# VectorE roots for the first and last norms, an early dummy partition maximum, and experts loaded in halves

## The chip, the cores and the metric

The kernel runs on one core of a Trainium2 chip. The metric is the device time of one execution in microseconds, and the figure given for a kernel is the median of its runs. The trace is of one further execution, recorded by the hardware profiler.

## What is computed

The reference applies four residual blocks to `x` (4 x 256 tokens of 128), each after a layer norm. Weights are 128 wide.

```
x = x + tanh(g_xattn[0]) * attention(norm(x), ctx)      # softmax(q k^T) v, 64 context rows a batch
x = x + tanh(g_ffn[0])   * experts(norm(x))             # 8 experts, the best 2 of each token, gelu
x = x + tanh(g_xattn[1]) * linear_attention(norm(x), ctx)   # 16 heads of 8, softmax over q and over k
x = x + tanh(g_ffn[1])   * quantised_ffn(norm(x))       # each stage scaled by max|.| over ALL tokens
norm(x) = (x - mean) / sqrt(var + 1e-5)
```

The layer norm needs one reciprocal square root for each token. The quantised block needs the largest absolute value of five whole tensors ("x", "g", "u", "p", "o") before it can go on with each.

## The kernel before

Every engine has its own instruction stream, written out by hand in order, and the engines meet only at semaphores. The 1024 tokens are worked on in two halves of 512 (4 tiles of 128), so a norm has a number n from 1 to 8: block (n-1)//2, half (n-1)%2.

A norm goes over four engines. VectorE computes `statistics` (bn_stats L557, bn_aggr L560, then var + eps, L562). GpSimd computes the root as a power of -1/2 in `rstd_of` (L311, a 128x4 tensor_tensor). VectorE takes `shift` (L568) and normalises two tiles (L573). ScalarE normalises the other two (L404). TensorE transposes them (`normalised`, L1000), and ScalarE copies them out (L395, or as `xhi` for the second block). `keep_warm` (L993) issues matmuls on zeros between.

The start: SyncE issues the DMAs of x half 0, packa, x half 1, packb, lpbq and experts (L275 to L280). GpSimd fills `ident`, `ones` and `neg_half`, makes the identity with an affine select (L316), and only then raises `const_ready`, on which TensorE waits with its first real matmul (L1070). VectorE runs the statistics of both halves, then both `normalise` calls (L685 to L689), then `weight_scales` (L586 to L590), `scores(0)` (L601, L602), `weight_values` (L595), `scores(1)`, then `add_attention` (L608 to L615) and the statistics of the second block.

Experts: ScalarE copies each of eight 128x512 expert blocks to a high part (`high_weights`, L410), and GpSimd subtracts that from the block (`low_weights`, L327). GpSimd's order is low_weights 0 to 6, rstd_of(3), low_weights 7, rstd_of(4), then the masks and constants (L335 to L350), and last `const_late`. VectorE's `route(0)` (L639 and on) waits for `const_late`; TensorE's `gate_columns` (L1144) waits for route, `first_rows` (L1151) for that, and the expert loop for those.

The end: GpSimd runs rstd_of(7), rstd_of(8) and then `partition_all_reduce` (L384) once for each of the five maxima. VectorE takes the maxima of the normalised tokens (L825) and of each partition (L840); the reduced maximum gives the scale (L879, L880), ScalarE rounds (L503), VectorE splits (L885, L887), and TensorE runs twelve units of three matmuls (L1013, L1014, L1017). ScalarE copies six of them (L508), and VectorE takes their maxima (L870).

Of the kernel before, what the change touches and what calls it, by code (L numbers as in the profile page):

```python
# [8 lines left out]
HALVES = 2  # L9
# [4 lines left out]
EXPERTS = 8  # L14
# [11 lines left out]
ROUND = 1.5 * 2.0 ** 23  # L26

# [10 lines left out]
def build(nc, x, packa, packb, rows, experts, lpbq, gates, out):  # L38
# [5 lines left out]
    i16, u16 = mybir.dt.int16, mybir.dt.uint16  # L44
# [5 lines left out]
    with ctx:  # L50
# [31 lines left out]
        ones = sb("ones", [128, 256])  # L82
        zero16 = sb("zero16", [128, 512], f16)
# [32 lines left out]

        smax = sb("smax", [128, HALVES, TILES])
# [60 lines left out]
        def third(t, dt=None):  # L178
# [30 lines left out]
        table_load = sb("table_load", [1, 2])  # L209


        x_in = [sem(f"x_in{h}") for h in range(HALVES)]
        pa_in, pb_in, row_in, exp_in, lpbq_in, out_done = map(
            sem, ("pa_in", "pb_in", "row_in", "exp_in", "lpbq_in", "out_done"))
        const_ready, const_late, pool_step = map(sem, ("const_ready", "const_late", "pool_step"))
        dve_step, zero_ready = map(sem, ("dve_step", "zero_ready"))
# [56 lines left out]
        def _(sp):  # L273
# [4 lines left out]
            sp.dma_start(pb[:, :], packb).then_inc(pb_in, 16)  # L278
            sp.dma_start(wq4[:, :, :], lpbq).then_inc(lpbq_in, 16)
            sp.dma_start(wexp[:, :], experts).then_inc(exp_in, 16)  # L280
# [16 lines left out]
        def _(pool):  # L297
# [7 lines left out]
            def link(ins):  # L305
                pool.wait_ge(pool_step, step(ins))

            def rstd_of(n):
# [4 lines left out]
            pool.memset(ident[:, :], 0.0)  # L313
            pool.memset(ones[:, :], 1.0)
            link(pool.memset(neg_half[:, :], -0.5))
            link(pool.affine_select(out=ident[:, :], in_=ident[:, :], compare_op=ALU.not_equal, fill=1.0,  # L316
                                    base=0, pattern=[[-1, 128]], channel_multiplier=1))
            pool.drain().then_inc(const_ready, 1)
            pool.memset(v1[:, :, D:D + 1], 1.0)
            pool.iota(number[:, :], pattern=[[1, EXPERTS]], base=0, channel_multiplier=0,  # L320
                      allow_small_or_imprecise_dtypes=True)
            rstd_of(1)
            rstd_of(2)
# [6 lines left out]
            for e in range(7):  # L330
                low_weights(e)
            rstd_of(3)
            low_weights(7)
            rstd_of(4)
            link(pool.memset(first_row[:, :], 0.0))  # L335
# [45 lines left out]
            rstd_of(8)  # L381
# [7 lines left out]
        def _(act):  # L389
# [18 lines left out]
            def high_weights(e):  # L408
                act.wait_ge(exp_in, 16)
                act.activation(w_hi[e], wexp[:, e * 512:(e + 1) * 512], ACT.Copy).then_inc(we_high, 1)  # L410
# [11 lines left out]
            high_weights(0)  # L422
            evac(half(xT, 1), bank[7][:, :], xT_mm, 2, xT_ready)
            for h in range(HALVES):
                act.wait_ge(s_sub, h + 1)
                act.activation(sc[:, h, :, :], sc[:, h, :, :], ACT.Exp).then_inc(pr_ready, 1)
                high_weights(1 + h)
                if h == 0:
                    evac(v0[:, :, :].rearrange("p b d -> p (b d)"), bank[3][:, 0:256], v0_mm, 1, v0_ready)
                evac(prT[:, h, :, :].rearrange("p t d -> p (t d)"), bank[2 + h][:, 0:256],  # L430
                     prT_mm, h + 1, prT_ready)
            for e in range(3, EXPERTS):
                high_weights(e)
# [105 lines left out]
        def _(dve):  # L539
# [10 lines left out]
            dve.memset(zero16[:, :], 0.0).then_inc(zero_ready, 1)  # L550
            dve.sem_inc(gated, CREDIT)
            dve.sem_inc(lo_done, CREDIT)

            def statistics(src, h):
# [7 lines left out]
                dve.tensor_scalar(var[:, h, :], mv[:, h, :, 1], LN_EPS, None, ALU.add).then_inc(var_ready, 1)  # L562

# [124 lines left out]
            normalise(xin, 1)  # L688
            normalise(xin, 2)  # L689
# [5 lines left out]
            weight_scales()  # L695
            dve.wait_ge(tg_ready, 1)
            scores(0)
            weight_values()
# [129 lines left out]
            statistics(x4, 1)  # L828
            dve.wait_ge(xn_ready, 7)
            dve.wait_ge(xn_act, 7)  # L830
            tokens_max(0, tiles(xn, 0))
            normalise(x4, 8)
# [151 lines left out]
        def _(pe):  # L984
# [90 lines left out]
            mm(bank[5][:, 0:256], A("wq", D), kT[:, :], start=True, stop=True).then_inc(wqk_mm, 1)  # L1075
            normalised(bank[6], 1)
# [229 lines left out]
```

## Time and profile before

| | us |
|---|---|
| median of 3 runs | 166.34 (166.28 to 167.22) |
| profiled execution, its own time | 166.24 |
| span of its trace | 164.5 |
| TensorE busy | 126.1 |
| VectorE busy | 127.0 |
| ScalarE busy | 94.0 |
| GpSimd busy | 34.0 |

The span runs from the first to the last recorded instruction; 1.74 us of the execution's own time lie outside it. Rows of the timeline give start, duration, engine, line, operation, output and input, count, and in brackets the idle time before them with what ended it. "issue" there means that the profile shows nothing that the engine waited for.

### The profile page before, as it was taken

To read this page: it belongs to the slowest core of one execution; us is meant where nothing else is said; L and a number is where in the kernel's file an instruction comes from. 1 tells how busy PE (TensorE), PEld (TensorE's weight loads), DVE (VectorE), ACT (ScalarE), POOL (GpSimd) and SP (SyncE) were. 2 spreads that over 40 slices of the span, in tenths; PEclk is the share of its full clock that TensorE was granted. 3 is DMA by queue.
4 is the path that set the end of the run, shared out by engine and by line. 5 is a ranking of instruction groups with operands and counts; after the bars stand their busy time and mean duration, and the time that the engine had idled before them with its cause. 6 is when DMAs were issued, how large, how long until landed. Compare 5 with 4: busy or idle time off the path is not lost.

```text
span 164.5 us, 2167 instructions
## 1 busy us (share of the span) xinstructions
PE 126.1 (77%) x684; PEld 95.4 (58%) x684; DVE 127.0 (77%) x335; ACT 94.0 (57%) x163; POOL 34.0 (21%) x64
## 2 busy tenths in 40 slices
PE   6139998499889999999999987989809950007792
PEld 4035865288448888888886756779607830005650
DVE  1608895747879999999998875878336799989894
ACT  3006692322778888888888945242433589491380
POOL 1041679593000000000000249624000000000000
PEclk9956999969999999999999999999965997555999
DMA  4990000000033214321300000000000000000003
GB/s 157 345 413 12 0 4 2 0 0 0 0 134 123 91 49 129 126 74 59 127 0 0 0 2 2 4 2 0 0 0 4 0 0 0 0 0 0 0 0 128
DMA packets 2957, 8.17 MB, mean 50 GB/s; under 512 B 249, under 2 KB 1273, under 8 KB 2818
## 3 DMA queue, kind: packets, MB, share of 16 engines
q1 hardware_dynamic: 2944, 8.03, 13.7%
q8 instruction: 5, 0.08, 0.2%
q14 instruction: 6, 0.05, 0.1%
q10 hardware_dynamic: 2, 0.00, 0.0%
HBM read 7.48 MB, written 0.56 MB: 49 GB/s over the span
## 4 chain that ended last, share of the span: by engine, by line
PE 35%; DVE 24%; issue 16%; POOL 15%; ACT 7%; POOLq 1%; DVEq 0%; ACTq 0%
PE bank L1013 9%; PE bank L1017 9%; PE bank L1014 9%; POOL we_lo L327 4%; POOL rstd L311 3%; DVE amax_u L870 2%; DVE hidden L902 2%; DVE amax_p L875 2%; DVE stats L557 2%; ACT wexp L531 2%; POOL q_soft L376 2%; POOL wT_lo L370 2%; PE bank L1151 1%; DVE amax_g L870 1%; DVE xn L573 1%
## 5 line engine op out<-in xcount | busy, mean ns | idle before, releaser
L993 PE MATMUL bank<-zero 128*128 128x256 f16 x199 | 30.8, 308 | 17.2 <-ACT ng L527 15.1
L993 PEld LDWEIGHTS bank<-zero 128*128 128x128 f16 x199 | 21.3, 110 | 24.8 <-ACT ng L527 15.5
L455 ACT ACTIVATE hidden<-bank 128x512 f32<-128x512 f32 x32 | 19.2, 598 | 6.5 <-PE bank L1017 6.5
L733 DVE TENSOR_TENSOR low_parts<-hidden,high_parts 128x512 fp32r<-128x512 f32 x32 | 21.9, 686 | 0.1
L311 POOL TENSOR_TENSOR rstd<-var,neg_half 128x4 f32<-128x4 f32 x8 | 8.1, 1018 | 63.8 <-DVE var L562 63.8
L460 ACT ACTIVATE high_parts<-hidden 128x512 fp32r<-128x512 f32 x32 | 20.0, 624 | 1.5 <-DVE hidden L726 1.4
L1017 PE MATMUL bank<-low_parts,we_hi 128*128 128x512 f32 x32 | 12.7, 396 | 0.7 <-DVE low_parts L733 0.6
L1013 PE MATMUL bank<-xhi,we_hi 128*128 128x512 f32 x32 | 12.8, 400 | 0.0
L1013 PE MATMUL bank<-high_parts,we_hi 128*128 128x512 f32 x32 | 12.7, 395 | 0.0
L1017 PE MATMUL bank<-xlo,we_hi 128*128 128x512 f32 x32 | 12.5, 390 | 0.0
L1014 PE MATMUL bank<-xhi,we_lo 128*128 128x512 f32 x32 | 12.5, 390 | 0.0
L1014 PE MATMUL bank<-high_parts,we_lo 128*128 128x512 f32 x32 | 12.5, 389 | 0.0
L726 DVE TENSOR_TENSOR hidden<-hidden,q_exp 128x512 f32<-128x512 f32 x16 | 11.1, 691 | 1.2 <-ACT q_exp L471 0.4
L327 POOL TENSOR_TENSOR we_lo<-wexp,we_hi 128x512 fp32r<-128x512 f32 x8 | 10.4, 1324 | 6.2 <-ACT we_hi L410 6.2
L726 DVE TENSOR_TENSOR hidden<-hidden,q_soft 128x512 f32<-128x512 f32 x16 | 11.1, 691 | 0.8
L568 DVE SCALAR_TENSOR_TENSOR shift<-mv,rstd 128x4 f32<-128x4 f32 x8 | 2.3, 284 | 9.5 <-POOL rstd L311 9.4
L1013 PE MATMUL bank<-xhi,wT_hi 128*128 128x512 f32 x12 | 5.8, 484 | 4.2 <-DVE xhi L885 4.2
L404 ACT ACTIVATE xn<-stream,shift,rstd 128x128 f32<-128x128 f32 x12 | 5.3, 485 | 6.6 <-DVE shift L568 6.5
L1000 PE MATMUL bank<-ident,xn 128*128 128x128 f32 x32 | 6.0, 298 | 3.8 <-DVE xn L573 3.6
L557 DVE BATCH_NORM_STATS2 stats<-stream 128x6 f32<-128x128 f32 x24 | 5.2, 280 | 3.6 <-DMA stream<-in_x 3.5
L1017 PEld LDWEIGHTS bank<-low_parts,we_hi 128*128 128x128 f32 x32 | 6.0, 188 | 2.7 <-DVE low_parts L733 1.5
L1000 PEld LDWEIGHTS bank<-ident,xn 128*128 128x128 f32 x32 | 3.9, 154 | 5.4 <-DVE xn L573 4.4
(225 smaller groups left out, 284.1 us busy)
## 6 DMA issues: line engine op xcount, KB each, us to landing
wexp<-in_experts SPq DMA_DIRECT2D x1, 2048.0 KB, 10.5
q_soft<-gates SPq DMA_DIRECT2D x4, 512.0 KB, 3.5
q_exp<-gates SPq DMA_DIRECT2D x3, 512.0 KB, 3.7
wq<-in_lpbq SPq DMA_DIRECT2D x1, 576.0 KB, 6.1
stream<-in_x SPq DMA_DIRECT2D x2, 256.0 KB, 3.7
out<-hidden SPq DMA_DIRECT2D x2, 256.0 KB, 2.1
pa<-in_packa SPq DMA_DIRECT2D x1, 325.0 KB, 3.3
pb<-in_packb SPq DMA_DIRECT2D x1, 256.0 KB, 4.8
```

Source lines behind the costliest of these rows:

```text
L311: pool.tensor_tensor(rstd[:, h, :], var[:, h, :], neg_half[:, :], ALU.pow).then_inc(rstd_ready, 1)
L327: pool.tensor_tensor(w_lo[e], wexp[:, e * 512:(e + 1) * 512], w_hi[e].bitcast(f32), ALU.subtract)\
L455: act.activation(ge[j % NB][:, :], bank[4 + j % NB][:, :], ACT.Gelu).then_inc(gelu_done, 1)
L460: act.activation(h_hi[j % NB][:, :], hm[j % NB][:, :], ACT.Copy).then_inc(hi_done, 1)
L557: m = step(dve.bn_stats(stats[:, h, t, :], src[:, h * TILES + t, :]))
L726: dve.tensor_tensor(hm[j % NB][:, :], ge[j % NB][:, :], half(gate_rows[(j // 4) % 2], (j // FC) % 2), ALU.mult)\
L733: dve.tensor_tensor(h_lo[j % NB][:, :], hm[j % NB][:, :], h_hi[j % NB][:, :].bitcast(f32), ALU.subtract).then_inc(lo_done, 1)
L993: mm(bank[b][:, 0:256], zero16[:, 0:128], zero16[:, 0:256], start=True, stop=True)
L1000: last = pe.transpose(dst[:, t * 128:(t + 1) * 128], src[:, h * TILES + t, :], ident[:, :])
L1013: mm(dst, whi, xh, start=start, stop=False)
L1014: mm(dst, wlo, xh, start=False, stop=False)
L1017: return mm(dst, whi, xl, start=False, stop=stop)
```

## The change

GpSimd no longer makes the identity; VectorE builds it in 32x32 blocks at the start and signals `ident_ready`, on which TensorE waits only ahead of `normalised(1)`. `const_ready` now comes with the memset of `ones`. The roots 1, 2 and 8 are computed on VectorE by nine small chained instructions; `normalise(1)` moves ahead of the statistics of half 1, and `normalise(8)` ahead of `tokens_max(0)`. A dummy `partition_all_reduce` on a constant tile stands between rstd_of(7) and the five real ones. The experts come in two DMAs, ahead of lpbq. GpSimd's low_weights are ordered 2, 3, 3 around rstd_of(3) and rstd_of(4), and GpSimd waits for `xn_ready` 3 and 4 ahead of the second and third group. ScalarE makes two high parts instead of one after each exponential. `weight_scales` moves behind `scores(0)`.

```diff
+MAGIC = float(0x5F3759DF)
+RS = 0.375 ** 0.5
...
 @@ sync
+            for k in range(2):
+                part = slice(k * EXPERTS * 256, (k + 1) * EXPERTS * 256)
+                sp.dma_start(wexp[:, part], experts[:, part]).then_inc(exp_in[k], 16)
             sp.dma_start(wq4[:, :, :], lpbq).then_inc(lpbq_in, 16)
-            sp.dma_start(wexp[:, :], experts).then_inc(exp_in, 16)
 @@ gpsimd
-            pool.memset(ident[:, :], 0.0)
-            pool.memset(ones[:, :], 1.0)
+            pool.memset(ones[:, :], 1.0).then_inc(const_ready, 1)
             link(pool.memset(neg_half[:, :], -0.5))
-            link(pool.affine_select(out=ident[:, :], in_=ident[:, :], compare_op=ALU.not_equal, fill=1.0,
-                                    base=0, pattern=[[-1, 128]], channel_multiplier=1))
-            pool.drain().then_inc(const_ready, 1)
             pool.memset(v1[:, :, D:D + 1], 1.0)
+            pool.memset(par_load[:, :], 1.0)
             pool.iota(number[:, :], pattern=[[1, EXPERTS]], base=0, channel_multiplier=0,
                       allow_small_or_imprecise_dtypes=True)
-            rstd_of(1)
-            rstd_of(2)
+            pool.wait_ge(const_ready, 1)
...
-            for e in range(7):
+            for e in range(2):
                 low_weights(e)
             rstd_of(3)
-            low_weights(7)
+            pool.wait_ge(xn_ready, 3)
+            for e in range(2, 5):
+                low_weights(e)
             rstd_of(4)
+            pool.wait_ge(xn_ready, 4)
+            for e in range(5, EXPERTS):
+                low_weights(e)
...
             rstd_of(7)
-            rstd_of(8)
+            pool.partition_all_reduce(par_load[:, 1:2], par_load[:, 0:1], 128, bass.bass_isa.ReduceOp.absmax)
 @@ scalar
-                act.wait_ge(exp_in, 16)
+                act.wait_ge(exp_in[2 * e // EXPERTS], 16)
...
-            high_weights(0)
...
-                high_weights(1 + h)
+                high_weights(2 * h)
+                high_weights(2 * h + 1)
...
-            for e in range(3, EXPERTS):
+            for e in range(4, EXPERTS):
 @@ vector
+            step(dve.memset(ident[:, :], 0.0))
+            link(dve.memset(one32[:, :], 1.0))
+            link(dve.tensor_tensor_scan(col32[:, :], one32[:, :], one32[:, :], 0.0, ALU.add, ALU.mult))
+            link(dve.transpose(prow32[:, :], col32[:, :]))
+            for q in range(0, 128, 32):
+                dve.tensor_tensor(ident[q:q + 32, q:q + 32], col32[q:q + 32, :], prow32[q:q + 32, :], ALU.is_equal)\
+                    .then_inc(ident_ready, 1)
...
+            def rstd_of(n):
+
+                h = (n - 1) % HALVES
+                v = var[:, h, :]
+                dve.wait_ge(var_ready, n)
+                link(dve.tensor_scalar(rs_y[0][:, :].bitcast(i32), v.bitcast(i32), -0.5, MAGIC, ALU.mult, ALU.add))
+                for k, out_ in enumerate((rs_y[1][:, :], rstd[:, h, :])):
+                    y = rs_y[k][:, :]
+                    link(dve.tensor_tensor(rs_v[:, :], y, y, ALU.mult))
+                    link(dve.scalar_tensor_tensor(out=rs_t[:, :], in0=rs_v[:, :], scalar=RS, in1=v,
+                                                  op0=ALU.mult, op1=ALU.mult))
+                    link(dve.scalar_tensor_tensor(out=rs_q[:, :], in0=rs_t[:, :], scalar=-10.0 * RS / 3.0,
+                                                  in1=rs_t[:, :], op0=ALU.add, op1=ALU.mult))
+                    last = dve.scalar_tensor_tensor(out=out_, in0=rs_q[:, :], scalar=5.0 * RS * RS, in1=y,
+                                                    op0=ALU.add, op1=ALU.mult)
+                    if k == 0:
+                        link(last)
+                last.then_inc(rstd_ready, 1)
...
                 statistics(xin, h)
-            normalise(xin, 1)
-            normalise(xin, 2)
+                rstd_of(1 + h)
+                normalise(xin, 1 + h)
...
-            weight_scales()
             dve.wait_ge(tg_ready, 1)
             scores(0)
+            weight_scales()
             weight_values()
...
             statistics(x4, 1)
+            rstd_of(8)
+            normalise(x4, 8)
             dve.wait_ge(xn_ready, 7)
             dve.wait_ge(xn_act, 7)
             tokens_max(0, tiles(xn, 0))
-            normalise(x4, 8)
 @@ tensor
+            pe.wait_ge(ident_ready, 4)
             normalised(bank[6], 1)
```

## Rows read from the trace of the kernel before

**Rows 1.** The chain of waits, by engine.
```profile
PE 35%; DVE 24%; issue 16%; POOL 15%; ACT 7%; POOLq 1%; DVEq 0%; ACTq 0%
```

**Rows 2.** Timeline, the start, up to the first normalised tokens.
```profile
1.18 0.10 POOL L315 MEMSET neg_half<- 128x4 f32 x1
4.71 0.38 DVE L560 BATCH_NORM_AGGREGATE mv<-stats 128x2 f32<-128x6 f32 x4
...
7.53 0.17 DVE L562 TENSOR_SCALAR var<-mv 128x4 f32<-128x4 f32 x1
10.30 0.28 POOL L316 TENSOR_SCALAR_AFFINE_SELECT ident<-ident 128x128 f32<-128x128 f32 x1 [9.02 <-issue]
...
13.11 0.60 DVE L573 TENSOR_SCALAR xn<-stream,mv,rstd 128x128 f32<-128x128 f32 x2
```

**Rows 3.** Timeline, VectorE's stretch of attention, and GpSimd's first two differences.
```profile
13.90 1.34 DVE L586 TENSOR_REDUCE wb_max<-wq 128x36 f32<-128x1152 f32 x1
...
15.91 1.36 DVE L590 TENSOR_TENSOR ng<-wq,wb_r 128x1152 int16<-128x1152 f32 x1
17.34 0.42 DVE L601 TENSOR_REDUCE smax<-bank 128x4 f32<-128x256 f32 x1
17.37 1.27 POOL L327 TENSOR_TENSOR we_lo<-wexp,we_hi 128x512 fp32r<-128x512 f32 x1 [4.38 <-ACT we_hi L410]
18.14 1.71 DVE L595 TENSOR_TENSOR wb_i<-ng,wb_s 128x1152 f32<-128x1152 int16 x1
20.25 0.42 DVE L601 TENSOR_REDUCE smax<-bank 128x4 f32<-128x256 f32 x1 [0.40 <-PE bank L1046]
21.49 0.18 DVE L609 RECIPROCAL smax<-ssum 128x4 f32<-128x4 f32 x1
21.70 0.23 DVE L610 TENSOR_SCALAR ssum<-smax,tg 128x4 f32<-128x4 f32 x1
24.45 0.26 DVE L562 TENSOR_SCALAR var<-mv 128x4 f32<-128x4 f32 x1
```

**Rows 4.** Timeline, GpSimd and the engines that wait for it, 22 to 39 us.
```profile
22.18 6.19 POOL L327 TENSOR_TENSOR we_lo<-wexp,we_hi 128x512 fp32r<-128x512 f32 x5 [1.20 <-ACT we_hi L410]
28.32 1.01 POOL L311 TENSOR_TENSOR rstd<-var,neg_half 128x4 f32<-128x4 f32 x1
29.30 1.26 POOL L327 TENSOR_TENSOR we_lo<-wexp,we_hi 128x512 fp32r<-128x512 f32 x1
29.44 1.14 DVE L568 SCALAR_TENSOR_TENSOR shift<-mv,rstd 128x4 f32<-128x4 f32 x1 [2.35 <-POOL rstd L311]
33.54 0.20 POOL L335 MEMSET first_row<- 8x128 f32 x1
38.50 0.19 DVE L639 COPY lg<-bank 128x32 f32<-128x32 f32 x1 [0.26 <-POOLq L351]
```

**Rows 5.** Windows: start and length, busy PE, PEld, DVE, ACT, POOL; clock, DMA share, GB/s.
```profile
12.00:13.00 1.00, 0.88 (x4) 0.15 (x1) 0.68 (x3) 0.51 (x2) 0.99 (x1) 0.50 0.35 148
...
28.00:30.00 2.00, 0.00 (x0) 0.00 (x0) 0.56 (x1) 0.00 (x0) 2.00 (x3) 1.00 0.00 0
32.00:34.00 2.00, 2.00 (x13) 1.44 (x11) 1.53 (x9) 0.72 (x2) 1.37 (x4) 0.54 0.00 0
120.00:121.00 1.00, 0.00 (x0) 0.00 (x0) 0.00 (x0) 0.00 (x0) 0.02 (x1) 0.95 0.00 0
127.00:128.00 1.00, 1.00 (x4) 0.78 (x3) 0.41 (x2) 0.60 (x1) 0.00 (x0) 0.64 0.00 0
```

**Rows 6.** Timeline, the last norm and the first maximum.
```profile
113.79 0.17 DVE L562 TENSOR_SCALAR var<-mv 128x4 f32<-128x4 f32 x1
114.04 1.01 POOL L311 TENSOR_TENSOR rstd<-var,neg_half 128x4 f32<-128x4 f32 x1 [2.27 <-DVE var L562]
116.71 0.16 DVE L840 TENSOR_REDUCE amax_x<-amax_x 128x1 f32<-128x3 f32 x1
120.98 0.41 POOL L384 PARTITION_ALL_REDUCE gmax_x<-amax_x  x1 [5.93 <-issue]
123.11 0.77 PE L1013 MATMUL bank<-xhi,wT_hi 128*128 128x512 f32 x1 [4.21 <-DVE xhi L885]
128.91 1.38 DVE L870 TENSOR_REDUCE amax_g<-stream 128x1 f32<-128x512 f32 x2 [0.27 <-ACT stream L508]
131.28 0.36 POOL L384 PARTITION_ALL_REDUCE gmax_g<-amax_g  x1 [9.89 <-DVE amax_g L840]
```

More of the change, by code:

```diff
@@ L43, in build @@
     f32, f32r, f16 = mybir.dt.float32, mybir.dt.float32r, mybir.dt.float16
-    i16, u16 = mybir.dt.int16, mybir.dt.uint16
+    i16, u16, i32 = mybir.dt.int16, mybir.dt.uint16, mybir.dt.int32
     ACT = mybir.ActivationFunctionType
@@ L82, in build @@
         ones = sb("ones", [128, 256])
+        one32 = sb("one32", [128, 32])
+        col32 = sb("col32", [128, 32])
+        prow32 = sb("prow32", [128, 32])
         zero16 = sb("zero16", [128, 512], f16)
@@ L115, in build @@
         xlo = sb("xlo", [128, TOKENS], f32r)
+        rs_y = [sb(f"rs_y{k}", [128, TILES]) for k in range(2)]
+        rs_v, rs_t, rs_q = (sb(f"rs_{k}", [128, TILES]) for k in "vtq")
         smax = sb("smax", [128, HALVES, TILES])
@@ L209, in build @@
         table_load = sb("table_load", [1, 2])
+        par_load = sb("par_load", [128, 2])
         x_in = [sem(f"x_in{h}") for h in range(HALVES)]
-        pa_in, pb_in, row_in, exp_in, lpbq_in, out_done = map(
-            sem, ("pa_in", "pb_in", "row_in", "exp_in", "lpbq_in", "out_done"))
+        exp_in = [sem(f"exp_in{k}") for k in range(2)]
+        pa_in, pb_in, row_in, lpbq_in, out_done = map(
+            sem, ("pa_in", "pb_in", "row_in", "lpbq_in", "out_done"))
         const_ready, const_late, pool_step = map(sem, ("const_ready", "const_late", "pool_step"))
-        dve_step, zero_ready = map(sem, ("dve_step", "zero_ready"))
+        dve_step, zero_ready, ident_ready = map(sem, ("dve_step", "zero_ready", "ident_ready"))
         kT_mm, kT_ready, v0_mm, v0_ready, g_mm, tg_ready = map(
```

## The prediction

> **What bounds the kernel now.** The reader is to look first at the chain of waits. TensorE and VectorE share most of it, but 16% of the span is "issue" and 15% is GpSimd [rows 1], although GpSimd is busy for only 34 of 164.5 us. So the order of GpSimd's few instructions matters. The timeline then shows where. At the start GpSimd stands still for 9.02 us ahead of its first affine select, with nothing it waits for [rows 2]; the first real matmul and both roots come after it. In the middle one queue carries the weight differences, the roots and the constants: root 3 starts at 28.32 though its variance was there at 24.71, and route starts at 38.50 when GpSimd's constants are done [rows 3, 4]. At the end GpSimd stands still again, 5.93 us ahead of its first partition reduce [rows 6]. The expert loop and everything behind it to 111 us touch nothing of the change, so a delay or a gain at 47 us is carried through whole. I therefore work out three stretches: up to the variance of norm 3, from there to route and the expert loop, and the last norm with its maximum.
>
> **Up to the variance of norm 3.** The nine root instructions are chained. Such a step costs 0.21 us (start 21.49 to 21.70 [rows 3]), so a root costs 9 x 0.21 = 1.9 us on VectorE, against 1.01 us on GpSimd [rows 4]. Bounds: 1.4 (0.16 each) to 2.4 (0.27, half again on the 0.18 of L609). The identity costs eight small instructions on VectorE, some 1.5 us, hidden in its wait for x until 3.80; without that cover it would delay all of the start by up to 1.5.
>
> Half 0: variance at 5.3 (the aggregates end at 5.09 [rows 2], plus 0.2), root to 7.2, shift and tokens 0.7, so 7.9. Half 1: statistics 1.5 to 9.4, root to 11.3, tokens to 12.0. Before, the tokens of half 1 end at 13.71 [rows 2]. So VectorE is 1.7 us ahead here, and half 0 is ahead by almost 5, which is of no use: VectorE is busy from here on. TensorE's chain (packa, kT, wqk, transposes) gives the first scores at about 11, before VectorE asks for them at 12.3.
>
> Then VectorE does the same work in another order, and the 0.40 us in which it waited for the second scores [rows 3] goes: 2.1 us ahead. The experts as two DMAs ahead of lpbq move the same bytes; the traffic is over in the window 12 to 13 [rows 5], and weight_scales asks for lpbq at 13.1, so I price this at nothing; if lpbq were the last by a microsecond, it would cost that microsecond here.
>
> Against it stands a lock. When GpSimd's difference began at 29.30, VectorE's shift at 29.44 took 1.14 us instead of 0.16 and ended with it [rows 4]. The same is in L595: 1.71 us beside a difference ending at 18.64, where L590, of the same size, took 1.36 [rows 3]. In the new order, ScalarE's first two high parts come at about 14.8 and 15.5, so the first two differences (1.25 each) fall on L590 (from 15.2) and L595. If each side waits for the other in turn, VectorE loses 1.0 and 1.25, less the 0.35 paid already: 1.9 of the 2.1 us. If L590 starts first, it loses about 1.1 less. I take 1.4: the variance of norm 3 is ready 0.7 us earlier, at 24.0. Bounds: 0 to 2.1.
>
> The Trainium skill says, in "SBUF — State Buffer", section "Who interferes with whom", that a VectorE instruction with two SBUF inputs and a GpSimd instruction that reads SBUF exclude each other for the whole instruction, and that issue order decides. The trace agrees (1.14 us for a shift that takes 0.16 alone). Without such a rule the variance would be ready at 22.6, and the forecast would be 1.4 us lower.
>
> **From that variance (V) to the expert loop.** Before, constants and route came at V + 13.8 (38.50 less 24.71 [rows 3, 4]). In the new order GpSimd runs: root 3 at once, to V + 1.05; then it waits for the tokens of norm 3. VectorE has add_attention(1) before them (about 2.0 without the stall) and 0.7 for the tokens: V + 2.7. Then three differences, 3.75 us (6.19 / 5 = 1.24 each [rows 4]): V + 6.5. Root 4, whose variance was ready at V + 4.2, runs to V + 7.5; tokens at V + 8.2. Three differences: V + 12.0. The constants, from 33.54 to 38.50 before, take 4.9 us [rows 4]: V + 16.9. So the differences, which lay ahead of root 3, now lie ahead of the constants, and route is 3.1 us later against V and, with the 0.7 gained, 2.4 us later in time: about 40.9. Nothing hides it: TensorE finishes the logits and two z units by about 37.5. Bounds: 1.0 (V early by 2.1) to 3.6 (no gain, and 0.5 of lock stalls from the keys' subtraction).
>
> That leaves TensorE idle for some 5 us before gate_columns(0). Of idle time the trace says: after nothing ran from 28 to 30, the clock is at 0.54 in 32 to 34, and after TensorE stopped at 118.9 it falls by 121 and is low until inside 127 to 128 [rows 5], 4.5 us behind the restart at 123.11. So here the transposes and the first copies of the gate rows run at 1.2 instead of 2.4 GHz. Before, these pieces take about 0.6 and 1.1 us on the path; doubled until some 4.3 us after the restart, they cost 0.8 us more (0 if the clock holds, 2.5 if all to the first gated unit is slow). Sum of the middle: 2.4 + 0.8 = 3.2 us later.
>
> **The last norm.** Root 7 stays on GpSimd and ends, on the old time axis, at 111.8. The dummy reduce then takes the stall. Before, the stall ran from the end of root 8 (115.05) to 120.98, 5.93 us [rows 6]; from 111.8 that gives 117.7, and with the dummy's own 0.4, 118.1. VectorE: variance at 113.96 [rows 6], root 1.9, shift and tokens 0.7, so 116.5; then all three token maxima, of which only two came after the tokens before: 0.69 + 0.44 + 0.44, and 0.16, so 118.2. The real reduce begins at 118.3 instead of 120.98: 2.7 us gained, and VectorE's maximum, 1.4 us later than the old 116.87, is what ends the wait. Bounds: 1.0 (the stall 1.7 longer) to 3.2 (root at 1.4).
>
> The Trainium skill, "GPSIMD Engine Reference", section "Instruction dispatch", puts about 6 us on the first call after a kernel library is loaded, with no instruction shown. The 5.93 us agree. By a reading in which that load began only when its input was ready, the stall would be 4.1 us (116.87 to 120.98), and the dummy is then done at 116.3, which changes no term.
>
> There is a second gain. TensorE's filler ends at about 119.6, and the quantised tokens reach it at 120.4, so it rests under 1 us instead of 4.2. With the clock held, its unit takes 0.69 instead of 1.28, and VectorE's maxima (0.69 each, as in the pair at 128.91 [rows 6]) set the pace. Before, from 123.11 to the reduce of g at 131.28 it took 8.2 us [rows 6]; now 0.95 for the first unit, 0.65 for its copy, 0.7 for the second half's split, six maxima at 0.69 partly beside these, and 0.2: 6.5. Gained 1.7 (0 if the clock falls all the same). Sum of the end: 4.4 us earlier.
>
> **Sum.** 3.2 - 4.4 = -1.2 us. The profiled execution had 166.24, the median is 166.34, 0.1 above it; the same step on the median gives 165.1.
>
> **Rivals.** (a) The middle costs little: the differences miss VectorE's two long instructions, so V is 2.1 earlier, and TensorE's clock holds. Then the middle is +1.0 and the sum -3.4: 162.9. For it: each stall depends on a few tenths in ScalarE's times. Against it: the three differences in front of the constants remain. (b) The end gives only the stall: the clock falls at 120 though the rest is short, so 1.7 are not gained: 166.8, no change. For it: the clock fell already 2 us after the last filler. Against it: here less than 1 us is idle. (c) Slower: GpSimd's chain of differences and constants. It starts with no gain in V, takes 0.5 of lock stalls (+3.6), and the expert loop starts with the clock low throughout (+2.5): +6.1, less 4.4: 168.1. It decides from a middle of over 6.1 us. For it: no other engine can shorten the chain. Against it: the clock would come back inside it. (d) The dummy does not hide the stall, because the stall there takes 9.0 us as at the start [rows 2]: then the reduce is at 121.2, the end gives nothing, and the time is 169.6. For it: the same kind of stall did take 9.0. Against it: DMA moved 400 GB/s then, and nothing here.
>
> **How the numbers follow.** The forecast has 0.44, (a) 0.28, (b) 0.16, (c) 0.07, (d) 0.05. A measurement of this kernel can tell about 1%, 1.66 us, from no change. Faster by over that (below 164.7): all of (a), and a quarter of the forecast, whose own range is 163.9 to 166.3: 0.39. Slower by over it (above 168.0): (d) and most of (c): 0.1. The rest, 0.51, is within. The range reaches from (a) to just above (b): 162.7 to 167.2.
>
> **What would show it.** Right: L316 gone, the iota first after a stall of about 9; nine VectorE instructions of about 0.21 each; the variance of norm 3 at 23 to 24.5; `const_late` and route at 40 to 41.5, with idle TensorE and a low clock before 43; the dummy reduce with the stall ahead of it, and the reduce of x straight behind amax_x; a clock of 1.0 through the first units of the last block. Wrong: a route at or before 38.5, which would make it rival (a) or better, or a stall ahead of the dummy that outlasts amax_x.

## The result and the profile after

The changed kernel takes 170.09 us (median of 4 runs, 168.48 to 170.76) against 166.69 (4 runs) for the kernel before on the same chip: ratio 1.0211 [1.0161, 1.0262]. It is slower by 1.6 to 2.6%, outside the range and on the other side than forecast. Here and below a ratio is against the kernel before on the same chip, with its 95% interval in brackets, and it leaves out the executions that are over 1.5% longer than the fastest of their kernel, which the medians take in. The profiled execution took 170.76 us, the longest of the four, with a span of 169.0 against 164.5, so the spans differ by 1.1 us more than the medians.

Cutting both spans at the same events shows where the 4.5 us of span came from (start times in the two timelines, us):

| stretch | before | after | difference | forecast |
|---|---|---|---|---|
| up to the variance of norm 3 ready (V) | 24.71 | 24.23 | -0.5 | -0.7 |
| V to route(0) | 13.8 | 18.2 | +4.4 | +3.1 |
| route(0) to the first matmul of the expert loop | 9.3 | 13.5 | +4.2 | +0.8 |
| expert loop and third block, to root 7 | 62.9 | 63.7 | +0.8 | 0 |
| root 7 to the reduce of g | 20.5 | 16.2 | -4.4 | -4.4 |
| reduce of g to the end | 33.2 | 33.2 | -0.1 | 0 |

The end gave back what was forecast. The middle, forecast at 3.2 us later by the start of the expert loop, is 8.2 later there (55.97 against 47.82), and 0.8 more is lost in a stretch that the change does not touch.

The page of the changed kernel, its chain by engine (which answers to [rows 1]) and the clock in 40 slices of 4.2 us:

```profile
PE 38%; DVE 23%; POOL 12%; issue 11%; DMA 6%; ACT 5%; SPq 2%; POOLq 1%; DVEq 0%
...
PEclk9999855997555799999999999999999998555999
```

"issue" and GpSimd went down by 5 and 3 points as intended; a DMA is on the chain now, and the clock shows two dips ahead of 60 us: slices 5 to 7, and 10 to 14. The timeline, start and attention, selected rows (to be read against [rows 2, 3]):

```profile
5.35 0.17 DVE L588 TENSOR_SCALAR rs_y<-var 128x4 int32<-128x4 int32 x1
...
6.93 0.17 DVE L596 SCALAR_TENSOR_TENSOR rstd<-rs_q,rs_y 128x4 f32<-128x4 f32 x1
...
10.88 0.14 POOL L328 IOTA number<- 128x8 f32 x1 [9.56 <-issue]
...
14.20 2.51 POOL L334 TENSOR_TENSOR we_lo<-wexp,we_hi 128x512 fp32r<-128x512 f32 x2 [3.17 <-ACT we_hi L422]
14.22 1.35 DVE L624 TENSOR_REDUCE wb_max<-wq 128x36 f32<-128x1152 f32 x1 [1.44 <-DMA wq<-in_lpbq]
15.61 1.13 DVE L626 TENSOR_SCALAR wb_s<-wb_max 128x36 f32<-128x36 f32 x1
...
17.19 1.36 DVE L628 TENSOR_TENSOR ng<-wq,wb_r 128x1152 int16<-128x1152 f32 x1
18.59 1.36 DVE L633 TENSOR_TENSOR wb_i<-ng,wb_s 128x1152 f32<-128x1152 int16 x1
19.86 0.42 DVE L639 TENSOR_REDUCE smax<-bank 128x4 f32<-128x256 f32 x1
...
21.24 0.69 PE L1092 MATMUL bank<-ident,sc 128*128 128x128 f32 x2 [4.70 <-ACT sc L437]
```

A root on VectorE takes nine steps from 5.35 to 7.10. GpSimd's stall of 9 us is still there, but only the iota stands behind it. Two things are new. VectorE waits 1.44 us for lpbq, and `wb_s` takes 1.13 us beside a difference, where the kernel before has

```profile
15.28 0.18 DVE L588 TENSOR_SCALAR wb_s<-wb_max 128x36 f32<-128x36 f32 x1
```

And TensorE waits 4.70 us for the second scores, which now stand behind both `weight_scales` and `weight_values` on VectorE. GpSimd's chain and what waits on it, selected rows (against [rows 4]):

```profile
24.06 0.17 DVE L581 TENSOR_SCALAR var<-mv 128x4 f32<-128x4 f32 x1
24.30 1.06 POOL L322 TENSOR_TENSOR rstd<-var,neg_half 128x4 f32<-128x4 f32 x1 [7.60 <-DVE var L581]
26.97 3.72 POOL L334 TENSOR_TENSOR we_lo<-wexp,we_hi 128x512 fp32r<-128x512 f32 x3 [1.61 <-DVE xn L611]
30.65 1.01 POOL L322 TENSOR_TENSOR rstd<-var,neg_half 128x4 f32<-128x4 f32 x1
32.55 0.69 DVE L662 TENSOR_TENSOR xlo<-bank,xhi 128x512 fp32r<-128x512 f32 x1 [4.25 <-ACT xhi L407]
33.22 0.60 DVE L611 TENSOR_SCALAR xn<-stream,mv,rstd 128x128 f32<-128x128 f32 x2
33.90 3.93 POOL L334 TENSOR_TENSOR we_lo<-wexp,we_hi 128x512 fp32r<-128x512 f32 x3 [2.24 <-DVE xn L611]
37.78 0.19 POOL L347 MEMSET first_row<- 8x128 f32 x1
42.43 0.19 DVE L677 COPY lg<-bank 128x32 f32<-128x32 f32 x1 [6.03 <-POOLq L363]
48.46 2.07 PE L1191 MATMUL bank<-gateT,first_row 8*128 8x512 f32 x2
52.28 2.07 PE L1191 MATMUL bank<-gateT,first_row 8*128 8x512 f32 x2
55.97 0.63 PE L1052 MATMUL bank<-high_parts,we_hi 128*128 128x512 f32 x1
```

The last row is the mark taken for the start of the expert loop in the table. In the kernel before it is

```profile
47.82 0.39 PE L1013 MATMUL bank<-high_parts,we_hi 128*128 128x512 f32 x1
```

Root 4 is done at 31.66, but its tokens only at 33.8: `xlo` of the half before stands ahead of them on VectorE and waits 4.25 us for `xhi`. Windows of after (columns as in [rows 5]) show why `xhi` is late, and what followed behind route:

```profile
20.00:25.00 5.00, 3.76 (x16) 2.30 (x16) 4.69 (x21) 3.80 (x8) 0.69 (x1) 0.50 0.02 3
25.00:30.00 5.00, 5.00 (x19) 3.56 (x20) 3.16 (x17) 1.42 (x4) 3.39 (x4) 0.50 0.00 0
30.00:35.00 5.00, 5.00 (x48) 4.55 (x47) 2.42 (x6) 1.48 (x3) 2.76 (x3) 0.99 0.00 0
35.00:40.00 5.00, 4.56 (x33) 3.62 (x31) 1.15 (x2) 0.90 (x2) 4.71 (x12) 1.00 0.00 0
40.00:45.00 5.00, 0.06 (x1) 0.10 (x2) 2.40 (x23) 0.21 (x1) 2.18 (x6) 0.53 0.00 0
45.00:50.00 5.00, 5.00 (x15) 2.35 (x14) 3.65 (x24) 2.67 (x4) 0.00 (x0) 0.50 0.00 0
50.00:55.00 5.00, 5.00 (x14) 2.19 (x14) 1.23 (x2) 2.20 (x4) 0.00 (x0) 0.50 0.31 111
```

TensorE was idle from 16.5 to 21.2, and in 20 to 30 its clock is at 0.50 (1.2 GHz). In its order the 20 fillers of norm 3 stand ahead of the transposes that `xhi` waits for; they start late and take 3.28 us, against 2.35 in the kernel before. First after, then before:

```profile
28.17 3.28 PE L1032 MATMUL bank<-zero 128*128 128x256 f16 x20
```

```profile
25.63 2.35 PE L993 MATMUL bank<-zero 128*128 128x256 f16 x20
```

Behind the second idle stretch, 39.6 to 44.9, the clock is at 0.50 for two whole windows in which TensorE never rests. The last norm, selected rows (against [rows 6]):

```profile
119.70 1.01 POOL L322 TENSOR_TENSOR rstd<-var,neg_half 128x4 f32<-128x4 f32 x1 [3.06 <-DVE var L581]
126.66 0.16 DVE L879 TENSOR_REDUCE amax_x<-amax_x 128x1 f32<-128x3 f32 x1
126.75 0.41 POOL L393 PARTITION_ALL_REDUCE par_load<-par_load  x1 [6.05 <-issue]
127.08 0.43 POOL L396 PARTITION_ALL_REDUCE gmax_x<-amax_x  x1
129.22 0.47 PE L1052 MATMUL bank<-xhi,wT_hi 128*128 128x512 f32 x1 [0.71 <-DVE xhi L924]
135.85 0.35 POOL L396 PARTITION_ALL_REDUCE gmax_g<-amax_g  x1 [8.35 <-DVE amax_g L879]
```

The dummy takes the stall, 6.05 us against 5.93, the real reduce follows at once, and TensorE waits 0.71 us instead of 4.21.

### The profile page after: what moved, and what is told of

It is laid out like the page before. It is cut to its first block, busy times and chain, and to the rows that moved or that the text cites. A ratio compares the mean times of both kernels' runs of the same rounds, so it can differ in the third digit from the quotient of the medians.

```text
span 169.0 us, 2201 instructions
## 1 busy us (share of the span) xinstructions
PE 133.7 (79%) x684; PEld 98.2 (58%) x684; DVE 132.6 (78%) x370; ACT 93.7 (55%) x163; POOL 30.5 (18%) x61
## 4 chain that ended last, share of the span: by engine, by line
PE 38%; DVE 23%; POOL 12%; issue 11%; DMA 6%; ACT 5%; SPq 2%; POOLq 1%; DVEq 0%
PE bank L1056 9%; PE bank L1052 9%; PE bank L1053 9%; DMA wq<-in_lpbq 6%; PE bank L1032 4%; PE bank L1191 2%; POOL we_lo L334 2%; DVE amax_u L909 2%; DVE amax_g L909 2%; DVE hidden L941 2%; DVE amax_p L914 2%; ACT wexp L543 2%; POOL rstd L322 2%; POOL q_soft L388 2%; POOL wT_lo L382 2%
## 5 line engine op out<-in xcount | busy, mean ns | idle before, releaser
L1032 PE MATMUL bank<-zero 128*128 128x256 f16 x199 | 31.8, 314 | 17.1 <-ACT ng L539 15.1
L322 POOL TENSOR_TENSOR rstd<-var,neg_half 128x4 f32<-128x4 f32 x5 | 5.1, 1021 | 72.1 <-DVE var L581 72.1
L1052 PE MATMUL bank<-xhi,we_hi 128*128 128x512 f32 x32 | 13.7, 427 | 0.0
L1056 PE MATMUL bank<-xlo,we_hi 128*128 128x512 f32 x32 | 13.2, 411 | 0.0
L1053 PE MATMUL bank<-xhi,we_lo 128*128 128x512 f32 x32 | 13.0, 407 | 0.0
L334 POOL TENSOR_TENSOR we_lo<-wexp,we_hi 128x512 fp32r<-128x512 f32 x8 | 10.2, 1294 | 7.0 <-DVE xn L611 3.8
L1052 PEld LDWEIGHTS bank<-xhi,we_hi 128*128 128x128 f32 x32 | 6.4, 201 | 1.5
L1056 PEld LDWEIGHTS bank<-xlo,we_hi 128*128 128x128 f32 x32 | 6.3, 197 | 1.6
L1053 PEld LDWEIGHTS bank<-xhi,we_lo 128*128 128x128 f32 x32 | 6.4, 199 | 1.2
L1052 PEld LDWEIGHTS bank<-high_parts,we_hi 128*128 128x128 f32 x32 | 6.1, 192 | 1.6 <-ACT high_parts L472 0.3
```

What stands on the lines that cost most here:

```text
L322: pool.tensor_tensor(rstd[:, h, :], var[:, h, :], neg_half[:, :], ALU.pow).then_inc(rstd_ready, 1)
L334: pool.tensor_tensor(w_lo[e], wexp[:, e * 512:(e + 1) * 512], w_hi[e].bitcast(f32), ALU.subtract)\
L1032: mm(bank[b][:, 0:256], zero16[:, 0:128], zero16[:, 0:256], start=True, stop=True)
L1052: mm(dst, whi, xh, start=start, stop=False)
L1053: mm(dst, wlo, xh, start=False, stop=False)
L1056: return mm(dst, whi, xl, start=False, stop=stop)
```

## The experiments

Starts are from the timeline of one execution of each kernel, "route" is the start of `route(0)`, and "y" the start of the expert loop as above. My theory after the result: the constants behind the differences make route late, and the idle time that this leaves costs again by the clock; the end is a pure gain. The main rival: the order of work before V, or the VectorE roots themselves, are to blame.

**tail_only**: the kernel before with the last norm's part alone (root 8 on VectorE, `normalise(8)` early, the dummy).

> The kernel before with the last norm's part of the change alone: root 8 on VectorE ahead of the token maxima, and the dummy reduce. The theory (the end is a gain of its own: 19.5 us from the end of root 7 to the reduce of g become 15.1 in the changed kernel): about 4.4 us faster than the kernel before, ratio 0.974, clock 1.0 through the first units of the last block. The rival (the end is faster in the changed kernel only because everything reaches it later, or the clock happened to be up there): under 2.8 us, ratio over 0.983.

Measured 162.92, ratio 0.9778 [0.9649, 0.9906]. Root 7 starts at 112.06, the dummy at 119.03, the reduce of g at 128.13: 16.1 us behind root 7, as in after. The part is worth 4.4 us of span, and the clock stays at 1.0:

```profile
116.00:121.00 5.00, 4.06 (x34) 2.98 (x31) 3.48 (x17) 2.64 (x6) 0.76 (x2) 1.00 0.00 0
121.00:126.00 5.00, 4.50 (x17) 3.08 (x18) 4.37 (x8) 3.04 (x6) 0.00 (x0) 1.00 0.01 3
```

**spread_undone**: after, with GpSimd's old order.

```diff
-            for e in range(2):
+            for e in range(7):
                 low_weights(e)
             rstd_of(3)
-            pool.wait_ge(xn_ready, 3)
-            for e in range(2, 5):
-                low_weights(e)
+            low_weights(7)
             rstd_of(4)
-            pool.wait_ge(xn_ready, 4)
-            for e in range(5, EXPERTS):
-                low_weights(e)
```

> The changed kernel with GpSimd's differences back in one row (0 to 6, root 3, 7, root 4) and without its two waits. The theory (the spreading puts the constants, and so route, behind the differences, and the wait lowers TensorE's clock): route near 38.5 again and the expert loop about 7 us earlier than the changed kernel's 54.6, so some 163 us, ratio 0.975 against the kernel before. The rival (VectorE's roots and the late weight scales cost the time): the middle keeps over half of its loss, ratio 1.00 or above.

Measured 162.98, ratio 0.9822 [0.9721, 0.9922]. V 23.67, route 37.46 (13.8 behind V, as before the change), y 46.78 (9.3 behind route). TensorE's clock is at 0.53 and 0.50 in 20 to 30 here too, and costs nothing on the way to route. So both middle terms, +4.4 and +4.2, belong to the spread differences with their two waits; roots, identity, experts in halves and the first norms' order are not slow by themselves.

**warm_wait**: after, with TensorE kept busy on zeros while it waits for route.

```diff
+            keep_warm(7, 48)
             gate_columns(0)
             z_unit(2, 2, 0)
```

> The changed kernel with 48 filler matmuls ahead of the first transposes of the gates, where TensorE stands idle for 5.4 us. The theory (of the 12.1 us from route to the expert loop 3.6 are the low clock): clock 1.0 from 40 to 55, the loop begins at about 51 instead of 54.6, ratio about 1.000 against the kernel before. The rival (that stretch is bound by VectorE and ScalarE, or the filler itself is in the way): it begins no earlier than 53.5, ratio 1.015 or more.

Measured 167.43, ratio 1.0058 [1.0016, 1.0099]. Route is no earlier (43.17), but y is at 52.51, 9.34 behind it, and the clock is at 1.00 from 35 on:

```profile
48.48 1.12 PE L1191 MATMUL bank<-gateT,first_row 8*128 8x512 f32 x2
50.52 1.12 PE L1191 MATMUL bank<-gateT,first_row 8*128 8x512 f32 x2
```

The pairs that took 2.07 take 1.12, with the same code. The 4.2 us behind route were the clock and nothing else. The span is 3.3 us shorter than that of after and not 4.2, since route came 0.7 later; by the ratios it is 1.5%, some 2.5 us. The stretch up to route varies as well: 18.9 us behind V here and in tail_undone, 18.2 in after, with the same code up to there.

**const_early**: after, with the masks and constants moved from behind the differences to behind the iota, where GpSimd waits anyway.

> The changed kernel with the masks and constants moved from behind the last difference to the stretch right behind the iota, where GpSimd waits for experts. The theory (the constants at the end of GpSimd's row gate route): route starts when the logits are done, at about 37 instead of 42.4, TensorE's clock does not fall, the loop starts at 45 to 46, 9 us earlier: ratio about 0.967 against the kernel before. The rival (logits and keys, or the third wait for we_lo, gate it as well): route at 40 or later, ratio over 0.985.

Measured 162.16, ratio 0.9743 [0.9641, 0.9845]. Route 37.56 (13.4 behind V), y 48.12, the differences still late. The order of constants behind differences is the whole of the +4.4: with it turned round route is 4.9 us earlier. TensorE still runs at 0.50 from 15 to 30, so the first dip alone does not bring the loss. Behind route the clock did fall, against the expectation (0.73 in 40 to 45): y is 10.6 us behind it instead of 9.3.

**before_again**: the kernel before, one further execution.

> The kernel before once more, for a second trace of it. In its first trace a matmul of the expert loop starts every 0.227 us, in those of the changed kernel and of four kernels made from it or from the one before every 0.233. If the pitch is a thing of the run or the chip: 0.233 here too, and 63.9 instead of 62.9 us from the first y matmul to root 7. If it hangs on the changed kernel's order: 0.227.

166.59 us, y to root 7 62.9 us again, where after has 63.7 and tail_only, spread_undone, warm_wait and const_early 63.9, so the difference is no chance of one execution. But route to y took 10.1 here (38.05 to 48.12) against 9.3 in the first trace: the clock term varies between executions of the same kernel.

**tail_undone**: after without the last norm's part.

> The changed kernel without its last norm's part: root 8 back on GpSimd, no dummy reduce. The theory (the end gives 4.4 us whatever comes before it): 4.4 us slower than the changed kernel, ratio about 1.047 against the kernel before. The rival (the end's gain hangs on what the rest of the change does to the clock): 1.035 or less.

Measured 173.24, ratio 1.0389 [1.0303, 1.0475]. By the sum it should stand at 1.021 + 0.026 = 1.047; both forecast and rival miss the median, and the interval takes in both. The trace settles it for the most part: root 7 to the reduce of g takes 20.0 us, against 16.2 with the part (20.5 in the kernel before). In this trace the clock came back earlier behind route: the pairs of first_rows take 1.12, route 43.27, y 53.83. So the second dip is worth some 4 us in one execution and 1.2 in another, and its size is no constant of the schedule.

**scores_first**: after, with `weight_scales` and `weight_values` behind the statistics of half 1, so that scores(1) come early.

```diff
             scores(0)
-            weight_scales()
-            weight_values()
             scores(1)
...
+            weight_scales()
+            weight_values()
             low_tokens(0)
```

> The changed kernel with the weight scales and values moved behind the second statistics of norm 4, so that the second scores wait for neither lpbq nor 4.5 us of weight work. The theory (TensorE rests from 16 to 21 because VectorE is at the weights, and its low clock from 20 to 30 then delays the copies to xhi and root 4's tokens): no idle over 2 us there, the variance of norm 3 at about 19.5, route at 37 to 38.5 since GpSimd's row behind norm 4 stays, some 4 to 5 us earlier than in the changed kernel and up to 8 with the clock: ratio 0.975 to 0.995. The rival (the weight work is on the path wherever it stands): within 1 us of the changed kernel, ratio 1.015 or more.

Measured 164.66, ratio 0.9847 [0.9744, 0.995], within the forecast and 3.6% below after. The trace does not show where that comes from: it is of an execution of 170.33 us, while three of the five took 163.48 to 164.66, so only its first 42 us are read. V is at 22.33, not 19.5, and route at 41.84. TensorE was at 0.50 in 15 to 25 although it was busy throughout, so the low clock there is not only the wait for scores(1). By the times, the place of the weight work is a second way to take back most of the loss with the constants left where they are; by which path stays open.

**best_a**: constants early, both roots straight and then six differences, scores first, the long quantisation products ahead of `xlo` and behind route.

> All that the runs so far suggest at once: the changed kernel with the constants right behind the iota, roots 3 and 4 straight after each other with the six differences behind them and no waits for tokens, the second scores ahead of the weight scales (these while VectorE waits for xhi, the values behind route). If the stretches add up: variance of norm 3 at about 19.5, route at about 30, the expert loop at 41 to 42 instead of 47.8, and 4.4 us less at the end: ratio about 0.935. If the differences of experts 2 to 7 or the lock between the two engines take it back: over 0.96.

Measured 164.33 (161.64 to 166.33; the kernel before beside it 167.3): 0.98 by the medians, the "over 0.96" of the expectation. V comes at 19.72, 4.5 us ahead of after, and over half of that is lost at once:

```profile
24.85 7.59 POOL L351 TENSOR_TENSOR we_lo<-wexp,we_hi 128x512 fp32r<-128x512 f32 x6
25.16 0.98 DVE L602 SCALAR_TENSOR_TENSOR shift<-mv,rstd 128x4 f32<-128x4 f32 x1
26.06 2.58 DVE L607 TENSOR_SCALAR xn<-stream,mv,rstd 128x128 f32<-128x128 f32 x2
```

Six differences in a row make `shift` and the tokens of norm 4 cost 3.5 us instead of 0.7. The two waits on `xn_ready` of the change keep the differences off just these, so they have their use; what costs is that the constants stand behind.

**pad_before, tail_only_last, const_early_last**: addresses alone. In after the loop's matmuls start 0.233 us apart, in the kernel before 0.227; the new small tiles stand ahead of `smax` and so move what is allocated behind. pad_before is the kernel before with an unused tile of 80 bytes there:

```diff
+        pad80 = sb("pad80", [128, 20])
         smax = sb("smax", [128, HALVES, TILES])
```

> The kernel before with one unused tile of 80 bytes a partition in the place where the changed kernel has its five root tiles, so that everything allocated after it (the parts of the expert loop among it) moves by 80 bytes. If the pitch of the loop's matmuls (0.227 us in both traces of the kernel before, 0.233 in all seven that have the root tiles there) hangs on these addresses: 0.233, 1.0 us more from the first y matmul to root 7, ratio about 1.006. If it hangs on the order of the instructions: 0.227, ratio 1.000.

Ratio 1.007 [1.0032, 1.0108] (12 runs, 167.86 against 166.81). Same program, same order, 80 bytes: y to root 7 goes from 62.9 to 63.6 us in the traces, which is 0.7 of the 1.2 us by which the times differ. Timeline of TensorE, first pad_before and then the kernel before:

```profile
70.02 0.40 PE L1014 MATMUL bank<-high_parts,we_hi 128*128 128x512 f32 x1
...
71.41 0.40 PE L1014 MATMUL bank<-high_parts,we_hi 128*128 128x512 f32 x1
```

```profile
70.45 0.39 PE L1013 MATMUL bank<-high_parts,we_hi 128*128 128x512 f32 x1
...
71.81 0.39 PE L1013 MATMUL bank<-high_parts,we_hi 128*128 128x512 f32 x1
```

Six matmuls take 1.39 us with the tile, 1.36 without it: 0.232 and 0.227 each.

> The kernel with the last norm's part alone, its five root tiles now allocated behind all others, so that the addresses before them are those of the kernel before. By the theory of addresses the pitch is 0.227 and it is 1.0 us faster than tail_only: ratio about 0.968. By the theory of order, no difference: 0.974 to 0.978.

With the new tiles allocated last: 162.51, 0.9757 [0.9709, 0.9806], spacing 0.227, y to root 7 63.0, against 63.9 in tail_only. The trace is as the theory of addresses has it, but the whole time is not: 0.9757 lies where the theory of order put it, the forecast 0.968 is outside the interval, and tail_only had 0.9778 [0.9649, 0.9906]. So the 0.9 us are shown in the loop, and in the whole time by pad_before alone.

> const_early with the new tiles allocated last. By the theory of addresses: pitch 0.227, 1.0 us less than const_early, ratio about 0.968. By the theory of order: as const_early, 0.974.

160.9, 0.963 [0.9562, 0.9699], spacing 0.227, y to root 7 62.95, against 63.9 in const_early. The ratio is below that of const_early (0.9743), but the two intervals overlap.

**best_c**: constants early, lpbq ahead of the experts, of the weight work only maximum, scale and reciprocal between the two scores, the two long products behind route and behind the keys' sum, tiles last; GpSimd does differences 0 and 1, both roots, and six differences behind xn 4.

> The lesson of best_a put right: constants right behind the iota; roots 3 and 4 straight after each other and the six differences only behind the tokens of norm 4 (in best_a they held VectorE up for 3 us at those tokens); lpbq ahead of the experts, so that maximum, scale and reciprocal of the weights fill VectorE's wait for the second scores; the two long weight products behind route(0) and behind the keys' sum; new tiles last. If stretches add up: variance of norm 3 near 19.8, route near 28 to 30, loop from 39 to 41, ratio 0.92 to 0.93. If the differences and the weight products again stand in the way of VectorE and TensorE's clock falls: loop from 45 or later, over 0.955.

Measured 162.78, 0.9682 [0.9595, 0.9769]: no better than const_early_last. The trace is of its longest execution, 163.68 us. V is at 22.2, but route(0) runs from 30.85 to 36.5, 5.7 us instead of 2.4, beside the six differences (28.36, 7.60 us): four of its instructions took 4.1 us together instead of 0.7, and the others what they take elsewhere. The clock is at 0.5 in 35 to 50.

**warm_both**: after, with fillers in both idle stretches.

```diff
             attend(0)
+            keep_warm(7, 40)
             attend(1)
...
+            keep_warm(7, 48)
             gate_columns(0)
```

> The changed kernel with filler matmuls in both of TensorE's idle times: 40 ahead of the second half's transposes of the first attention (idle 16.5 to 21.2), 48 ahead of those of the gates (39.6 to 44.9). The theory (1.3 us between the variance of norm 3 and route, and 4.2 behind route, are the low clock): clock 1.0 from 20 to 55, xhi some 3 us earlier, route 16.9 us behind the variance instead of 18.2, the first y matmul 9.3 us behind route: ratio about 0.995 to 1.000. The rival (GpSimd's row alone sets the 18.2): as warm_wait, 1.006, route 18 us or more behind the variance.

Measured 166.18 (10 runs), 0.9954 [0.9903, 1.0005]. V is where it was (24.17), `xlo` starts at 30.67 instead of 32.55, and the chain behind it follows:

```profile
30.67 0.69 DVE L662 TENSOR_TENSOR xlo<-bank,xhi 128x512 fp32r<-128x512 f32 x1 [2.43 <-ACT xhi L407]
...
32.40 3.92 POOL L334 TENSOR_TENSOR we_lo<-wexp,we_hi 128x512 fp32r<-128x512 f32 x3 [0.79 <-DVE xn L611]
```

Route (40.93) is 16.8 us behind V, y (50.26) 9.33 behind route. The group of three differences starts at V + 8.2 and route comes at V + 16.8, as the forecast had both. So with the clock at 1.00 in every window of 5 us from 15 to 60 but one (0.66 in 25 to 30), the schedule's own arithmetic stands. The whole comes to 166.2 against 165.1 forecast, and the loop's spacing is 0.8 of the rest. The rival, that GpSimd's row alone sets the 18.2, is out.

**best_d**: best_c, with the differences put where no long VectorE instruction was expected beside them, and six fillers. The edit against after, in part in words:

```diff
@@ gpsimd (constants behind the iota)
+            for e in range(4):
+                low_weights(e)
+            rstd_of(3)
+            pool.wait_ge(xn_ready, 3)
+            low_weights(4)
+            rstd_of(4)
+            pool.wait_ge(xn_ready, 4)
+            for e in range(5, 7):
+                low_weights(e)
+            pool.wait_ge(gate_ready, 2)
+            low_weights(7)
@@ scalar: high parts 0 to 3 at the first exponential, 4 at the second
@@ vector: as best_c. sync: lpbq ahead of experts. tiles last
@@ tensor
+            keep_warm(7, 6)
             gate_columns(0)
```

> best_c with the differences of experts 0 to 3 made while GpSimd waits for norm 3, 4 between the two roots, 5 and 6 behind norm 4's tokens and 7 only behind route, and six filler matmuls ahead of the gates' transposes. If the lock on route is what took best_c's gain: route(0) 2.3 us long, the first y matmul near 41, ratio about 0.93. If the low clock of the start is: route(0) at 2.3 to 3 us, but the loop from 44 or later, 0.95 to 0.965.

Measured 157.66 (157.21 to 158.26), ratio 0.9481 [0.9374, 0.9588]: faster than both kernels.

```profile
14.77 4.97 POOL L351 TENSOR_TENSOR we_lo<-wexp,we_hi 128x512 fp32r<-128x512 f32 x4 [0.18 <-ACT we_hi L423]
...
30.61 0.19 DVE L682 COPY lg<-bank 128x32 f32<-128x32 f32 x1
...
36.59 1.27 POOL L351 TENSOR_TENSOR we_lo<-wexp,we_hi 128x512 fp32r<-128x512 f32 x1 [5.50 <-DVE gate L704]
36.76 2.31 DVE L638 TENSOR_TENSOR wb_i<-ng,wb_s 128x1152 f32<-128x1152 int16 x1
```

Route(0) is at 30.61, no longer waits for GpSimd at all, and takes 2.4 us; y is at 42.88, 13 us ahead of after. So the lock on route was a cost of best_c. The ratio and y fall between the two expectations (0.93 with y near 41, 0.95 to 0.965 with y from 44): the clock still fell, to 0.53 in 40 to 45. Differences still meet the keys' subtraction (28.68, 1.27 us instead of 0.42) and a long product (2.31 us instead of 1.36).

## Why the prediction was wrong

**Start: size right, by two errors that cancel.** V came at 24.23 against a forecast of 24.0. The root took 1.8 us (forecast 1.9), the identity was done at 2.73, inside VectorE's wait for x, and VectorE was at `weight_scales` by 12.8, 0.3 ahead of the forecast. But "The experts as two DMAs ahead of lpbq ... I price this at nothing" was wrong: lpbq landed last and cost 1.44. I had named the price of a microsecond but took no account of it in the sum. By that delay the 1.4 us taken for the lock on the two long products did not come: they started at 17.19 and 18.59, behind the two differences, which ended at 16.71, and ran their 1.36. The lock hit the small `wb_s` instead (1.13, against 0.18 for the same instruction before). In numbers: 24.0, less 0.3, less the 1.4 and the 0.35 of lock that the kernel before had paid, plus 1.44 and 0.95, gives 24.3.

**V to route: "root 4 ...; tokens at V + 8.2" failed.** The counts of GpSimd's work were right: its instructions took 3.72, 1.01, 3.93 and 4.65 us. The tokens came at V + 9.6, because normalise(4) stands behind low_tokens(0) in VectorE's order and that one waits for TensorE's transposes. I had walked GpSimd's queue and left out what the instruction that it waits for is queued behind. And what stands ahead of those transposes in TensorE's order ran at 0.50 in 20 to 30, since TensorE had stood idle from 16.5 to 21.2: the move of `weight_scales` in between the two scores was counted only as 0.40 us gained for VectorE, and never as a wait of TensorE. warm_both tests just this: with filler in that gap the clock is at 1.00 in 15 to 25, and route is at V + 16.8. The delay reaches route only through GpSimd's row with the constants at its end: spread_undone and const_early have the low clock too, and route 13.8 and 13.4 behind V.

**Clock behind route: "they cost 0.8 us more" was mis-sized.** It measured 4.2, above even the bound of 2.5 (warm_wait gives all of it back). I had taken the time to return from one place, 4.5 us behind a restart [rows 5, 6]. Here TensorE restarted at 44.94 and was at 0.50 until 55, and at 0.76 in the window from 55 to 60. And I had counted too few pieces: against warm_wait the stretch up to the pairs costs 0.7 more, the two pairs 1.9, the eight fillers between them 0.8, and the fillers and the unit behind them 0.7. All of it is on the path, fillers too, since they stand in TensorE's order. The time of the return is not fixed either: tail_undone, with a like idle stretch, had its full clock already for first_rows.

**Middle as a whole.** It came out at +8.2 at y, beyond rival (c)'s 6.1. That rival named the right chain, differences and constants and then a low clock, and had 0.07. Of its two other conditions one did not hold (V had its 0.5), and the stall of the keys' subtraction did come, 1.27 us instead of 0.42, but cost GpSimd's three differences only 0.2. What made the rival too small and too unlikely was its price for the clock, from the same short low-clock rows.

**Expert loop: "touch nothing of the change" failed by 0.8.** The instructions are the same, their addresses are not. pad_before shows that the address alone does this.

**Last norm: right in both terms.** The stall was 6.05 (forecast 5.93), so the reduce of x came right behind amax_x, 7.4 us behind the start of root 7 instead of 10.2: 2.8 gained, forecast 2.7. The clock held, and from TensorE's first unit to the reduce of g it took 6.6 us instead of 8.2: 1.5 gained, forecast 1.7. With the rest 4.4 us, and tail_only measures 3.7 us [1.6, 5.8] of the whole time by its ratio. One detail differs: the dummy ended 0.3 behind amax_x, not before it. Rivals (b) and (d) are out. Rival (a), that the middle costs little, is out too.

**Sum.** Forecast +3.2 - 4.4 = -1.2; the traces show +8.2 + 0.8 - 4.4 - 0.1 = +4.5. The medians differ by 3.4. The other executions of after were shorter than the traced one, and where they lost less is not known.

## What to carry to other kernels

When an instruction is moved behind a wait, walk the queue of the engine waited for as well, with what that queue waits for in turn; and when a consumer is moved behind other work, price the idle time of its producer by the clock, at the longest low stretch that any trace shows and not at the shortest. Constants that depend on nothing belong where an engine stands still anyway: that move alone took this change from 1.021 to 0.974, and with the new tiles put last it was at 0.963. In this kernel new small tiles are best put last in memory, so that the addresses of the loop's operands stay.

## What the runs showed that was not expected

An unused tile of 80 bytes makes a kernel 0.7% slower, and 0.7 of the 1.2 us come from the loop, where matmuls of 512 columns start 0.232 instead of 0.227 us apart. All nine other traces with the new tiles ahead of `smax` have 0.232 or 0.233, and the four with tiles allocated last 0.227. Which operand's address decides, and why, was not tried and stays open.

After the same idle stretch the clock came back at different times: low through first_rows (2.07 us a pair) in after, full there (1.12) in tail_undone; and in best_d 6 short fillers did not prevent 0.53 in 40 to 45. What decides this was not settled.

A difference on GpSimd stalls instructions of one input too: `wb_s` (L626), a tensor_scalar of 36 elements, took 1.13 instead of 0.18 us. The forecast had quoted only half of the rule. The same was to be seen in the kernel before, where L610, a tensor_scalar that takes its scalar from a tile, took 0.66 us beside the row of differences that starts at 22.18 [rows 4], against 0.23 alone [rows 3]:

```profile
25.28 0.66 DVE L610 TENSOR_SCALAR ssum<-smax,tg 128x4 f32<-128x4 f32 x1
```

It came again in best_a (`wb_s`, 1.11) and in best_c (a tensor_scalar of route, 1.27 instead of 0.16). The Trainium skill ("SBUF — State Buffer", section "Who interferes with whom") says beside it that `tensor_scalar` can enter a mode that takes both ports, and then locks in the same way; the 1.13 us agree, though no run here tells that from another cause. The long products, which I had expected to be hit, came behind the differences in after and ran their 1.36; in best_d, where wb_i started 0.17 us behind one, it took 2.31.
